# One product for the group moments of two layers in each step of the loop, in place of two

## The chip, the cores and the metric

The kernel runs on one core of a Trainium2 chip. The time is device time in microseconds (us) of one execution on that core. Smaller is better.

## The reference

The input x is 32 images of 16 x 16 tokens with 256 channels, float32. Two residual layers follow each other, each on a group norm of its input (32 groups of 8 channels, with mean and variance over all tokens and channels of a group):

```python
def _gn(v, G=32, eps=1e-05):
    g = v.reshape(B_, H_, W_, G, C_ // G)
    m = jnp.mean(g, axis=(1, 2, 4), keepdims=True)
    s = jnp.var(g, axis=(1, 2, 4), keepdims=True)
    return ((g - m) / jnp.sqrt(s + eps)).reshape(v.shape)

x = x + _L0_conv_ref(_gn(x), ...)
x = x + _L1_conv_ref(_gn(x), ...)
```

Layer 0 is attention in shifted 8 x 8 windows with 16 heads, normalized queries and keys, a position bias, a mask and a softmax. Layer 1 is linear attention with 16 heads, once along the columns of an image (a = 0) and once along the rows (a = 1), and the two results are summed.

## The kernel before

**Layout.** An image lies as [128 channels, 2 x 256 tokens]. Precision comes from pairs of float16 numbers, a high and a low part: ScalarE (ACT) writes the high part, VectorE (DVE) or GpSimd (POOL) the low part (`low`, L1372, and others), and TensorE (PE) multiplies in three passes.

**The order of the work.** Nothing is scheduled by a program. Each engine has its own list of calls, written by hand, with its own waits on semaphores. In the middle each engine runs `step(k)`, which works on about seven images at once, each at another stage: image k enters, image k-1 is in the window attention, k-3 and k-4 in the axial attention, k-6 leaves. PE runs `step(k)` for k = 6 to 31, 26 steps. Hand-ordered lists stand ahead of it and behind it. `reach(eng, sem, img, per, j)` is a wait for the semaphore's count for an image; `edge` is the same wait, but only for the first and the last eight images.

**The group moments.** For an image and a layer, `group_stats` (L1544) and `group_moments` (L1551 to L1554) on DVE leave 12 numbers per channel in `stat[layer]`. `group_means` (L714) on PE multiplies them by the 128 x 128 float32 matrix `group8`, which sums over the eight channels of a group, into 12 columns of a PSUM bank: bank 0 for layer 0, bank 2 for layer 1. `group_var` on DVE reads these sums (L1561) and makes the variance in three more small instructions (L1564, L1566, L1568). `rstd` on POOL (L1377) takes the power -1/2. `group_norm` on DVE (L1580, two instructions for each layer) writes the normalized image in float32.

**One step of PE around it** (L742 to L769): `axial_out(0)` (L661, L662), `group_means(0)` of image k after a wait for `kv_copied[1]` (ACT, L1023), `axial_y` (L672), `group_means(1)` of image k-2, `scores` (L591), `axial_q(1)` and `axial_q(0)` (L559), `axial_out(1)` (L661, L662) after a wait for `biased[1]`, `window_den` (L600), `window_pv` (L609) after a wait for `y_added`, `window_qk` (L559).

**DVE in the same stretch** (end of its step and start of the next): `o1_sum(0)` (L1600), `group_var(0)`, `group_var(1)`, `add_bias` twice (L1660, after the scores), `group_norm(0)`, `group_norm(1)` (L1580), `add_x1` (L1706, L1708), which signals `y_added`.

**POOL in the same stretch** (L1408 to L1423): `rstd(1)`, `rstd(0)`, `token_low(1)` (L1372, kv<-kv, 128 x 1024), `normed_low(0)`:

```python
                for img in there(k - 2):
                    rstd(1, img)
                for img in there(k):
                    rstd(0, img)
                for img in there(k - 3):
                    token_low(1, img)
```

Of the kernel before, what the change touches and what calls it, by code (L numbers as in the profile page):

```python
# [14 lines left out]
P = 128  # L15
# [28 lines left out]
def image(n):  # L44

    return Image(n, n % 2, n // 2, n % 4)


def earlier(img, by):
    return image(img.n - by)  # L50
# [6 lines left out]
def missing(n):  # L57
    return not 0 <= n < IMAGES


def reach(eng, sem, img, per=1, j=None):

    if not missing(img.n):
        eng.wait_ge(sem, img.n * per + (per if j is None else j))
# [10 lines left out]
def placed(usual, moved):  # L75

    return lambda img: moved.get(img.n, usual)


def edge(eng, sem, img, per=1, j=None):  # L80

    if img.n < EDGE or img.n >= IMAGES - EDGE:
        reach(eng, sem, img, per, j)
# [24 lines left out]
def build(nc, x, Wq, Wk, Wv, bv, Wo, bo, logit_scale, cpb_w1, cpb_b1, cpb_w2, w_qkv0, w_out0, w_qkv1, w_out1,  # L108
          c_ident, c_group, c_small, c_mask, c_coords, out, scratch):
    ctx = ExitStack()  # L110
    with ctx:
        def sb(name, shape, dt=F32):
            return ctx.enter_context(nc.sbuf_tensor(name, shape, dt))

        def sem(name):
            return ctx.enter_context(nc.semaphore(name))
# [3 lines left out]
        group8 = sb("group8", [P, P])  # L120
# [20 lines left out]

        x_in = sb("x_in", [P, 2, 2, D])
        x_t = sb("x_t", [P, 2, HALF])
        stat = [sb(f"stat{l}", [P, 32]) for l in range(2)]
        xn32 = [sb(f"xn32_{l}", [P, HALF]) for l in range(2)]
        xn = [sb(f"xn{l}", [P, 2, HALF], F16) for l in range(2)]
        xn1 = [sb("xn_cols", [P, 2, HALF], F16), xn[1]]
# [26 lines left out]
        ps = ctx.enter_context(nc.psum_tensor("ps", [P, 8, 512], F32))  # L174
# [32 lines left out]
        xt_copied = sem("xt_copied")  # L207
        gn_small = [sem(f"gn_small{l}") for l in range(2)]
        gn_sum = [sem(f"gn_sum{l}") for l in range(2)]
        gn_pow = [sem(f"gn_pow{l}") for l in range(2)]  # L210
        xn_hi = [sem(f"xn_hi{l}") for l in range(2)]
        xn_lo = [sem(f"xn_lo{l}") for l in range(2)]
# [16 lines left out]
        v_ready = sem("v_ready")  # L229
# [20 lines left out]
        kv_copied = [sem(f"kv_copied{a}") for a in range(2)]  # L250
# [15 lines left out]

        GN_STEPS = 11
        LATE = 3

        QK_BANK = placed(6, {0: 1, 1: 4})  # L270
        V_BANK = placed(2, {0: 7})
# [16 lines left out]
        GM_BANK = (placed(0, {}),  # L288
                  placed(2, {}))
# [48 lines left out]
        def gram_place(g, s):  # L338

            return 16 * (s // 4 % 2) + 8 * g + 4 * (s // 8) + s % 4  # L340
# [20 lines left out]
        def there(k):  # L361

            img = image(k)
            return [] if missing(img.n) else [img]
# [158 lines left out]
        def _(pe):  # L523
# [130 lines left out]
            def axial_out(a, img):  # L654
                reach(pe, gram_spread[a], img, 64)
                for s in range(G * SEQ):
                    cols = slice(s * SEQ, (s + 1) * SEQ)
                    dst = ps[:, O_BANK[a](img) + s // SEQ, (s % SEQ) * 2 * SEQ:(s % SEQ + 1) * 2 * SEQ]
                    at = gram_place(*divmod(s, SEQ))
                    high, low = (gram_wide[a][:, at, :, :, gp].rearrange("p h e -> p (h e)") for gp in range(2))  # L660
                    pe.matmul(dst.rearrange("p (t i) -> p t i", t=2), high, q1[a][:, :, cols], start=True, stop=False)  # L661
                    last = pe.matmul(dst[:, 0:SEQ], low, q1[a][:, 0, cols], start=False, stop=True)  # L662
                last.then_inc(o1_done[a], 1)

            def axial_y(img):
                reach(pe, o1_lo[1], img)
                for g in range(G):
                    n = 0
                    for a in range(2):
                        for c2 in range(2):  # L670
                            for wp, xp in PASSES:
                                last = pe.matmul(ps[:, Y_BANK(img), g * TOK:(g + 1) * TOK],  # L672
                                                 w_l1[a]["o"][:, wp, c2, g * P:(g + 1) * P],
                                                 o1[a][:, xp, c2 * TOK:(c2 + 1) * TOK],
                                                 start=(n == 0), stop=(n == 11))
                                n += 1
                last.then_inc(y_proj, 1)
# [34 lines left out]
            def group_means(layer, img):  # L712
                reach(pe, gn_small[layer], img, GN_STEPS, 5)
                pe.matmul(ps[:, GM_BANK[layer](img), 0:12], group8[:], stat[layer][:, 0:12],  # L714
                          start=True, stop=True).then_inc(gn_sum[layer], 1)

            def step(k):
                for img in there(k - 4):
                    reach(pe, o1_summed[1], earlier(img, 1))
                    gram_matmuls(0, img)  # L720
                for img in there(k - 3):
                    reach(pe, o_scaled, earlier(img, -1))
                    axial_kv(0, img)
                for img in there(k - 2):
                    window_out(img)
                for img in there(k - 4):
                    reach(pe, gram_lo[0], img)
                    gram_matmuls(1, img)
                for img in there(k - 1):
                    window_v(img)  # L730
                for img in there(k):
                    reach(pe, z_ready, earlier(img, 2))
                    image_channels(img)
                for img in there(k - 3):
                    reach(pe, kv_hi[0], img)
                    axial_kv(1, img)
                for img in there(k - 6):
                    reach(pe, qk_scaled, earlier(img, -5))
                    edge(pe, y_copied, earlier(img, 1))
                    result_rows(img)  # L740
                for img in there(k - 4):
                    reach(pe, xt_copied, earlier(img, -4))  # L742
                    edge(pe, qk_scaled, earlier(img, -3))
                    axial_out(0, img)
                for img in there(k):
                    reach(pe, kv_copied[1], earlier(img, 3))
                    group_means(0, img)
                for img in there(k - 5):
                    edge(pe, kv_copied[1], earlier(img, -2))
                    axial_y(img)  # L750
                for img in there(k - 2):
                    reach(pe, v_ready, earlier(img, -1))
                    group_means(1, img)
                for img in there(k - 1):
                    reach(pe, o1_summed[0], earlier(img, 3))
                    reach(pe, y_copied, earlier(img, 5))
                    scores(img)
                for img in there(k - 3):
                    reach(pe, gn_small[0], earlier(img, -3), GN_STEPS, 6)
                    axial_q(1, img)  # L760
                    reach(pe, gn_small[1], earlier(img, -1), GN_STEPS, 6)
                    axial_q(0, img)
                for img in there(k - 4):
                    reach(pe, biased[1], earlier(img, -3))
                    axial_out(1, img)
                for img in there(k - 1):
                    window_den(img)
                    reach(pe, y_added, earlier(img, 4))
                    window_pv(img)  # L769
                for img in there(k):  # L770
                    window_qk(img)
# [199 lines left out]
        def _(act):  # L971
# [25 lines left out]
            def value_bias_high():  # L997
                act.wait_ge(late_in, 16 * LATE)
                act.activation(bv_two[:, 0, :], bv_col[:], ACT.Copy, scale=WS).then_inc(bv_hi, 1)
# [478 lines left out]
        def _(dve):  # L1478
# [43 lines left out]
            def bias_tables():  # L1522

                dve.wait_ge(rows_in, 16 * 16)
                dve.wait_ge(late_in, 16 * LATE)
                for w in range(NW):
# [29 lines left out]
            def group_var(layer, img):  # L1556

                s, done = stat[layer], gn_small[layer]
                reach(dve, gn_sum[layer], img)
                means = ps[:, GM_BANK[layer](img), 0:12].rearrange("p (g h v) -> p g v h", h=2, v=3)  # L1560
                dve.tensor_reduce(s[:, 20:24].rearrange("p (g v) -> p g v", v=2), means[:, :, 1:3], AXES.X,  # L1561
                                  ALU.add).then_inc(done, 1)
                reach(dve, done, img, GN_STEPS, 6)
                dve.tensor_tensor(s[:, 24:26], s[:, 20:24:2], s[:, 20:24:2], ALU.mult).then_inc(done, 1)  # L1564
                reach(dve, done, img, GN_STEPS, 7)
                dve.tensor_tensor(s[:, 30:32], s[:, 21:24:2], s[:, 24:26], ALU.subtract).then_inc(done, 1)  # L1566
                reach(dve, done, img, GN_STEPS, 8)
                dve.tensor_scalar(s[:, 26:28], s[:, 30:32], 0.0, GN_EPS, ALU.max, ALU.add).then_inc(done, 1)  # L1568
# [385 lines left out]
```

## Time and profile before

| | |
|---|---|
| time, median of 3 runs | 896.25 us (895.89 to 896.89) |
| profiled execution, its own time | 903.6 us |
| its span | 901.4 us |
| PE busy | 844.6 us (94%) |
| DVE busy | 736.4 us (82%) |
| ACT busy | 662.7 us (74%) |
| POOL busy | 480.2 us (53%) |
| granted TensorE clock, mean | 0.978 of full speed |

The span goes from the first to the last instruction of the profiled execution. Busy shares are averages over a start, 26 like steps of 25.5 to 26.6 us each, and an end.

### The profile page before, as it was taken

What the parts mean: (1) busy time and instruction counts of PE and PEld (TensorE: products, weight loads), DVE (VectorE), ACT (ScalarE), POOL (GpSimd) and SP (SyncE); (2) the same over time, 40 slices, a digit from 0 to 9 for tenths busy, and PEclk for the clock granted to TensorE, in tenths of its full rate; (3) what the DMA queues carried; (4) which work ended last, traced back from release to release, by engine and by line L of the source; (5) the groups of instructions that cost most, each with busy time, mean ns of one, the idle gap of its engine ahead of it and who ended that gap; (6) DMA issues with size and microseconds to landing.
All of it is one profiled execution on the core that took longest, in us unless ns stands there. A gap on an engine that the chain in (4) does not pass through costs nothing.

```text
span 901.4 us, 45971 instructions
## 1 busy us (share of the span) xinstructions
PE 844.6 (94%) x20128; PEld 659.9 (73%) x20128; DVE 736.4 (82%) x1536; ACT 662.7 (74%) x1108; POOL 480.2 (53%) x358
## 2 busy tenths in 40 slices
PE   5477899999999999999999999999999999999876
PEld 3354677778788777778787777778777778787655
DVE  7879888888889888888898888888888888887452
ACT  3656777877777778777777787777877877777542
POOL 4445455665655555655655556565565655654220
PEclk9699999999999999999999999999999999999988
DMA  6101434343344443343444443334444343334453
GB/s 165 58 13 36 80 75 81 66 88 78 80 83 92 92 91 82 84 82 81 81 89 92 89 84 81 78 79 87 88 91 92 77 87 77 74 72 94 78 108 83
DMA packets 334430, 74.04 MB, mean 82 GB/s; under 512 B 282372, under 2 KB 333718, under 8 KB 334230
## 3 DMA queue, kind: packets, MB, share of 16 engines
q1 hardware_dynamic: 322128, 69.53, 37.2%
q8 instruction: 158, 2.59, 1.3%
q10 hardware_dynamic: 12102, 1.59, 1.1%
q14 instruction: 42, 0.34, 0.1%
HBM read 12.31 MB, written 8.40 MB: 23 GB/s over the span
## 4 chain that ended last, share of the span: by engine, by line
PE 76%; SPq 7%; DVE 6%; issue 4%; ACT 3%; DMA 2%; POOL 1%; ACTq 1%; DVEq 0%; POOLq 0%
PE ps L559 20%; PE ps L629 15%; PE ps L672 8%; PE ps L661 6%; PE ps L650 6%; PE ps L576 4%; PE ps L662 3%; PE ps L600 3%; PE ps L591 3%; PE ps L609 3%; SPq L439 3%; SPq L429 2%; PE ps L714 1%; PE ps L708 1%; DMA gram_wide<-gram 1%
## 5 line engine op out<-in xcount | busy, mean ns | idle before, releaser
L1372 POOL TENSOR_TENSOR kv<-kv,kv 128x1024 f16<-128x1024 f32 x60 | 128.6, 2144 | 87.1 <-ACT kv L1018 84.3
L1082 ACT ACTIVATE probs<-probs 128x1024 f32<-128x1024 f32 x64 | 67.8, 1059 | 89.5 <-DVE probs L1660 87.4
L1377 POOL TENSOR_TENSOR stat<-stat,small 128x2 f32<-128x2 f32 x64 | 43.3, 693 | 135.5 <-DVE stat L1568 127.8
L661 PEld LDWEIGHTS ps<-q,gram_wide 128*128 128x128 f16 x2048 | 107.2, 97 | 10.9 <-DVE probs L1660 4.9
L661 PE MATMUL ps<-q,gram_wide 128*128 128x32 f16 x2048 | 111.3, 176 | 3.2 <-DMA gram_wide<-gram 2.6
L662 PE MATMUL ps<-q,gram_wide 128*128 128x16 f16 x2048 | 110.4, 169 | 0.0
L662 PEld LDWEIGHTS ps<-q,gram_wide 128*128 128x128 f16 x2048 | 106.0, 97 | 0.4
L559 PE MATMUL ps<-xn,w_q 128*128 128x256 f16 x768 | 98.3, 279 | 6.5 <-POOL xn L1372 6.5
L1594 DVE SCALAR_TENSOR_TENSOR gram<-ps,small,gram 128x512 f16<-128x512 f32 x128 | 94.6, 794 | 8.0 <-ACT gram L1035 5.1
L1372 POOL TENSOR_TENSOR xn<-xn,xn 128x512 f16<-128x512 f32 x64 | 74.9, 1171 | 48.7 <-ACT xn L1071 48.7
L1035 ACT ACTIVATE gram<-ps,small 128x512 f16<-128x512 f32 x128 | 95.4, 818 | 4.4 <-PE ps L650 4.4
L672 PE MATMUL ps<-o,w_o 128*128 128x256 f16 x768 | 90.7, 275 | 2.7 <-DVE o L1606 2.7
L629 PE MATMUL ps<-w_kv,xn 128*128 128x512 f16 x384 | 89.5, 383 | 1.0 <-ACT kv L1023 1.0
L1372 POOL TENSOR_TENSOR qk<-qk 128x1024 f16<-128x1024 f32 x32 | 68.9, 2154 | 38.8 <-ACT qk L1102 38.8
L629 PE MATMUL ps<-w_kv,xn_cols 128*128 128x512 f16 x384 | 88.4, 380 | 0.7 <-DVE o L1600 0.5
L1660 DVE TENSOR_TENSOR probs<-ps,bias_mask 128x1024 f32<-128x1024 f32 x64 | 75.5, 1220 | 14.5 <-PE ps L591 14.5
L559 PEld LDWEIGHTS ps<-xn,w_q 128*128 128x128 f16 x768 | 71.7, 100 | 20.1 <-POOL xn L1372 5.0
L672 PEld LDWEIGHTS ps<-o,w_o 128*128 128x128 f16 x768 | 76.1, 102 | 12.1 <-DVE o L1606 2.9
L1618 DVE STREAM_TRANSPOSE qk<-qk_sq 128x1024 f32<-128x1024 f32 x32 | 39.9, 1245 | 48.4 <-ACT qk_sq L1087 48.4
L1372 POOL TENSOR_TENSOR xn_cols<-xn,xn_cols 128x512 f16<-128x512 f32 x32 | 45.3, 1415 | 58.8 <-ACT xn_cols L1077 58.8
L650 PE MATMUL ps<-v_wide,kv 64*32 64x128 f16 x6144 | 69.2, 224 | 7.5 <-issue 3.7
L650 PEld LDWEIGHTS ps<-v_wide,kv 64*32 64x32 f16 x6144 | 58.8, 90 | 22.3 <-issue 21.1
(124 smaller groups left out, 1976.4 us busy)
## 6 DMA issues: line engine op xcount, KB each, us to landing
gram_wide<-gram SPq DMA_DIRECT2D x248, 128.0 KB
v_wide<-kv SPq DMA_DIRECT2D x496, 32.0 KB
x_in<-x SPq DMA_DIRECT2D x32, 128.0 KB, 2.4
x_in<-x SPq DMA_DIRECT2D x64, 64.0 KB, 2.3
out<-y_out SPq DMA_DIRECT2D x32, 128.0 KB
out<-y_out SPq DMA_DIRECT2D x64, 64.0 KB
gram_wide<-gram ACTq DMA_DIRECT2D x8, 128.0 KB
x<-L_conv_w_qkv SPq DMA_DIRECT2D x1, 768.0 KB, 4.5
```

Of the source, the lines that this page charges most:

```text
L559: last = pe.matmul(dst, w[:, wp, c, m * P:m * P + P], act[:, xp, c * TOK:(c + 1) * TOK], start=(n == 0), stop=(n == 5))
L629: last = pe.matmul(ps[:, KV_BANK[a](img) + t, :], xn1[a][:, xp, c * TOK + t * P:c * TOK + t * P + P], w_l1[a]["kv"][:, wp, c, :], start=(n ...
L650: last = pe.matmul(dst.rearrange("p (s e) -> p s e", e=32), kv[a][rows, kp, t, own], v_wide[a][rows, :, vp, t, own], start=(n == 0), stop= ...
L661: pe.matmul(dst.rearrange("p (t i) -> p t i", t=2), high, q1[a][:, :, cols], start=True, stop=False)
L662: last = pe.matmul(dst[:, 0:SEQ], low, q1[a][:, 0, cols], start=False, stop=True)
L672: last = pe.matmul(ps[:, Y_BANK(img), g * TOK:(g + 1) * TOK], w_l1[a]["o"][:, wp, c2, g * P:(g + 1) * P], o1[a][:, xp, c2 * TOK:(c2 + 1) * ...
L1035: last = act.activation(gram_half(a, head, 0), gram_psum(a, head, img), ACT.Copy, scale=gram_mask[:, head:head + 1])
L1082: act.activation(part, part, ACT.Exp).then_inc(probs_ready[g], 1)
L1372: return pool.tensor_tensor(dst, whole, high, ALU.subtract)
L1377: pool.tensor_tensor(stat[layer][:, 28:30], stat[layer][:, 26:28], minus_half, ALU.pow).then_inc(gn_pow[layer], 1)
L1594: last = dve.scalar_tensor_tensor(gram_half(a, head, 1), gram_psum(a, head, img), gram_mask[:, head:head + 1], gram_half(a, head, 0), ALU. ...
L1660: dve.tensor_tensor(probs[:, 4 * g:4 * g + 4, :].rearrange("p a n -> p (a n)"), ps[:, S_BANK[g](img):S_BANK[g](img) + 2, :].rearrange("p b ...
```

## The change

Both `stat` buffers become one tensor. In PE's `step`, k = 6 to 31, one product `both_group_means` of 24 columns takes the place of the two products of 12; it writes bank 2, where the layer 1 product stood, behind `axial_y`. DVE's `group_var` of both layers waits for it. Products in the hand-ordered lists stay as they are. The wait for `kv_copied[1]` moves to `axial_y`, and the wait of `axial_q(1)` for the layer 0 reader of bank 0 goes.

```diff
-        stat = [sb(f"stat{l}", [P, 32]) for l in range(2)]
+        stat_both = sb("stat", [P, 2, 32])
+        stat = [stat_both[:, l] for l in range(2)]
...
+        TOGETHER = range(6, 32)
+        TOGETHER_BANK = 2
...
+            def both_group_means(img):
+
+                reach(pe, gn_small[0], img, GN_STEPS, 5)
+                reach(pe, gn_small[1], earlier(img, 2), GN_STEPS, 5)
+                pe.matmul(ps[:, TOGETHER_BANK, 0:24], group8[:], stat_both[:, :, 0:12],
+                          start=True, stop=True).then_inc(both_sum, 1)
...
+                for img in there(k - 5):
+                    reach(pe, kv_copied[1], earlier(img, -2))
+                    axial_y(img)
                 for img in there(k):
-                    reach(pe, kv_copied[1], earlier(img, 3))
-                    group_means(0, img)
-                for img in there(k - 5):
-                    edge(pe, kv_copied[1], earlier(img, -2))
-                    axial_y(img)
-                for img in there(k - 2):
-                    reach(pe, v_ready, earlier(img, -1))
-                    group_means(1, img)
+                    reach(pe, v_ready, earlier(img, 1))
+                    both_group_means(img)
...
                 for img in there(k - 3):
-                    reach(pe, gn_small[0], earlier(img, -3), GN_STEPS, 6)
                     axial_q(1, img)
...
-                reach(dve, gn_sum[layer], img)
-                means = ps[:, GM_BANK[layer](img), 0:12].rearrange("p (g h v) -> p g v h", h=2, v=3)
+                k = img.n + 2 * layer
+                if k in TOGETHER:
+                    dve.wait_ge(both_sum, k - TOGETHER.start + 1)
+                    sums = ps[:, TOGETHER_BANK, 12 * layer:12 * layer + 12]
+                else:
+                    dve.wait_ge(gn_sum[layer], k - 2 * layer + 1 if k < TOGETHER.start else k - 2 * layer + 1 - len(TOGETHER))
+                    sums = ps[:, GM_BANK[layer](img), 0:12]
+                means = sums.rearrange("p (g h v) -> p g v h", h=2, v=3)
```

PE in one step, from the product of layer 0 to the first `axial_q`. `ps` is PSUM, `o_0` and `o_1` are the two axial results, `gn_small` counts DVE's small steps of the norm. Before:

```order
L714 MATMUL ps<-stat,group 128x12 [waits gn_small0,kv_copied1]
L672 MATMUL ps<-o_0,w_o 128x256 [waits o1_lo1]
L672 MATMUL ps<-o_0,w_o 128x256 x5
L672 MATMUL ps<-o_1,w_o 128x256 x6
L672 MATMUL ps<-o_0,w_o 128x256 x6
L672 MATMUL ps<-o_1,w_o 128x256 x6
L714 MATMUL ps<-stat,group 128x12 [waits gn_small1,v_ready]
L591 MATMUL ps<-qk,k_two 128x64 [waits y_copied,o1_summed0]
L591 MATMUL ps<-qk,k_two 128x64 x95
L559 MATMUL ps<-xn,w_q 128x256 [waits gn_small0]
```

The same place in the changed kernel, whose lines have other numbers (L676 is `axial_y`, L725 the new product, L595 `scores`):

```order
L676 MATMUL ps<-o_0,w_o 128x256 [waits o1_lo1,kv_copied1]
L676 MATMUL ps<-o_0,w_o 128x256 x5
L676 MATMUL ps<-o_1,w_o 128x256 x6
L676 MATMUL ps<-o_0,w_o 128x256 x6
L676 MATMUL ps<-o_1,w_o 128x256 x6
L725 MATMUL ps<-stat,group 128x24 [waits gn_small1,gn_small0,v_ready]
L595 MATMUL ps<-qk,k_two 128x64 [waits y_copied,o1_summed0]
L595 MATMUL ps<-qk,k_two 128x64 x95
L563 MATMUL ps<-xn,w_q 128x256 x12
```

The layer 0 product ahead of `axial_y` is gone, and the one product left stands behind `axial_y`, with the waits of both.

DVE from `o1_sum(0)` to the bias, before (`group_var(0)` is the first four small instructions, `group_var(1)` the next four):

```order
L1600 TENSOR_TENSOR o_32_0<-ps,o_32_0 128x512 [waits o1_aside0]
L1561 TENSOR_REDUCE stat<-ps 128x4 [waits gn_sum0]
L1564 TENSOR_TENSOR stat<-stat 128x2 [waits gn_small0]
L1566 TENSOR_TENSOR stat<-stat 128x2 [waits gn_small0]
L1568 TENSOR_SCALAR stat<-stat 128x2 [waits gn_small0]
L1561 TENSOR_REDUCE stat<-ps 128x4 [waits gn_sum1]
L1564 TENSOR_TENSOR stat<-stat 128x2 [waits gn_small1]
L1566 TENSOR_TENSOR stat<-stat 128x2 [waits gn_small1]
L1568 TENSOR_SCALAR stat<-stat 128x2 [waits gn_small1]
L1660 TENSOR_TENSOR probs<-ps,bias_mask 128x1024 [waits pv_done,den_done,scores_done] x2
```

The same place in the changed kernel (L1613 is `o1_sum(0)`, L1574 the read of the sums):

```order
L1613 TENSOR_TENSOR o_32_0<-ps,o_32_0 128x512 [waits o1_aside0]
L1574 TENSOR_REDUCE stat<-ps 128x4 [waits both_sum]
L1577 TENSOR_TENSOR stat<-stat 128x2 [waits gn_small0]
L1579 TENSOR_TENSOR stat<-stat 128x2 [waits gn_small0]
L1581 TENSOR_SCALAR stat<-stat 128x2 [waits gn_small0]
L1574 TENSOR_REDUCE stat<-ps 128x4 [waits both_sum]
L1577 TENSOR_TENSOR stat<-stat 128x2 [waits gn_small1]
L1579 TENSOR_TENSOR stat<-stat 128x2 [waits gn_small1]
L1581 TENSOR_SCALAR stat<-stat 128x2 [waits gn_small1]
L1673 TENSOR_TENSOR probs<-ps,bias_mask 128x1024 [waits pv_done,den_done,scores_done] x2
```

No instruction of DVE has moved; the first of the two reads now waits for the common product, `both_sum`.

## Rows read from the trace of the kernel before

**Rows 1.** Page, part 1, and windows view of steps k = 6 to 30

```profile
PE 844.6 (94%) x20128; PEld 659.9 (73%) x20128; DVE 736.4 (82%) x1536; ACT 662.7 (74%) x1108; POOL 480.2 (53%) x358
...
152.50:796.40 643.90, 641.52 (x15704) 506.65 (x15701) 550.92 (x1176) 508.28 (x851) 371.03 (x276) 1.00 0.41 84
```

**Rows 2.** Waits from 152 to 796 us: total us, times, longest

```profile
POOL stat L1377 <- DVE stat L1568: 89.7, 23, 4.8
...
DVE stat L1561 <- PE ps L714: 12.5, 25, 1.0
...
DVE probs L1660 <- PE ps L591: 9.2, 25, 0.5
...
PEld ps L609 <- DVE y L1708: 6.8, 22, 0.4
PEld ps L661 <- DVE probs L1660: 4.7, 20, 0.3
```

**Rows 3.** Timeline of PE's weight loads, one step: start, duration

```profile
408.61 0.30 PEld L714 LDWEIGHTS ps<-stat,group 128*128 128x128 f32 x2
408.74 2.61 PEld L672 LDWEIGHTS ps<-o,w_o 128*128 128x128 f16 x24
411.36 0.30 PEld L714 LDWEIGHTS ps<-stat,group 128*128 128x128 f32 x2
411.69 0.85 PEld L591 LDWEIGHTS ps<-qk,k_two 32*128 32x128 f16 x96
...
417.92 0.95 PEld L609 LDWEIGHTS ps<-probs,v_diag 128*32 128x32 f32 x64 [0.27 <-DVE y L1708]
418.96 0.55 PEld L559 LDWEIGHTS ps<-xn,w_q 128*128 128x128 f16 x6
...
434.25 0.30 PEld L714 LDWEIGHTS ps<-stat,group 128*128 128x128 f32 x2
```

**Rows 4.** Timeline of DVE, the same step

```profile
410.64 0.16 DVE L1561 TENSOR_REDUCE stat<-ps 128x4 f32<-128x8 f32 x1
...
411.80 0.17 DVE L1561 TENSOR_REDUCE stat<-ps 128x4 f32<-128x8 f32 x1 [0.40 <-PE ps L714]
...
412.39 0.17 DVE L1568 TENSOR_SCALAR stat<-stat 128x2 f32<-128x2 f32 x1
412.96 2.36 DVE L1660 TENSOR_TENSOR probs<-ps,bias_mask 128x1024 f32<-128x1024 f32 x2 [0.40 <-PE ps L591]
...
417.59 0.27 DVE L1708 SCALAR_TENSOR_TENSOR y<-ps,x 128x128 f32<-128x128 f32 x1
```

**Rows 5.** Timeline of POOL, the same step

```profile
412.64 1.34 POOL L1377 TENSOR_TENSOR stat<-stat,small 128x2 f32<-128x2 f32 x2 [3.78 <-DVE stat L1568]
413.94 2.14 POOL L1372 TENSOR_TENSOR kv<-kv,kv 128x1024 f16<-128x1024 f32 x1
```

**Rows 6.** First L1580 of two steps, POOL in the second; then both at the start

```profile
415.23 1.00 DVE L1580 TENSOR_SCALAR xn<-x_t,stat 128x256 f32<-128x256 f32 x1
...
261.46 0.88 DVE L1580 TENSOR_SCALAR xn<-x_t,stat 128x256 f32<-128x256 f32 x1
...
260.05 2.14 POOL L1372 TENSOR_TENSOR kv<-kv,kv 128x1024 f16<-128x1024 f32 x1
...
75.28 0.73 DVE L1580 TENSOR_SCALAR xn<-x_t,stat 128x256 f32<-128x256 f32 x2
```

**Rows 7.** Timeline of DVE, a hand-ordered pair of group_var at the start

```profile
52.50 0.17 DVE L1561 TENSOR_REDUCE stat<-ps 128x4 f32<-128x8 f32 x1
...
53.17 0.16 DVE L1561 TENSOR_REDUCE stat<-ps 128x4 f32<-128x8 f32 x1
```

**Rows 8.** Timeline of ACT, the copy that signals kv_copied[1], the same step

```profile
407.53 1.02 ACT L1023 ACTIVATE kv<-ps 128x1024 f32<-128x1024 f32 x1
```

**Rows 9.** Timeline of PE's weight loads, a step whose scores came late

```profile
263.30 0.59 PEld L600 LDWEIGHTS ps<-probs,small 128*32 128x32 f32 x16
264.03 1.07 PEld L609 LDWEIGHTS ps<-probs,v_diag 128*32 128x32 f32 x64
265.19 0.88 PEld L559 LDWEIGHTS ps<-xn,w_q 128*128 128x128 f16 x9
```

More of the change, by code:

```diff
@@ L209, in build @@
         gn_sum = [sem(f"gn_sum{l}") for l in range(2)]
+        both_sum = sem("both_sum")
         gn_pow = [sem(f"gn_pow{l}") for l in range(2)]
```

## The prediction

> **What bounds the kernel now.** I read the page's busy line first, then the windows view of the loop. Over the whole span PE is busy 94%. In the loop it is busy 641.52 of 643.90 us, at a granted clock of 1.00 (its level of 2.4 GHz) [rows 1]. So PE seems to be the bound, and work taken from it seems to be time gained. Matmul records overlap and their ends are modelled, so I check this in the waits. There PE's weight loads wait for two things in nearly every step: `window_pv` (L609) for DVE's `y` in 22 steps, 6.8 us in all, and `axial_out(1)` (L661) for DVE's `probs`, 4.7 us [rows 2]. PE is full, but DVE hands it its work just in time.
>
> Next I follow one step on three engines. PE loads for the layer 0 product at 408.61, for `axial_y` at 408.74, for the layer 1 product at 411.36, for `window_pv` at 417.92, and the next step's first product is at 434.25: a period of 25.64 us [rows 3]. DVE reads the layer 0 sums at 410.64, long after their product, because it was busy; it then stands idle 0.40 us for the layer 1 sums, reads them at 411.80 and ends `group_var(1)` at 412.39 + 0.17 = 412.56 [rows 4]. POOL's two `rstd` start at 412.64, right behind that, and `token_low(1)` at 413.94, until 416.08 [rows 5]. POOL waits for L1568 in the same way 23 times, 89.7 us in all [rows 2].
>
> **The link that decides** is the next one. The first L1580 of `group_norm(0)` starts at 415.23 and takes 1.00 us, where two of them take 0.73 us with no kv subtraction of POOL beside them [rows 6]. It ends at 416.23, 0.15 us after POOL's kv instruction. In the step whose bias came late it starts later and takes only 0.88 us, until 262.34, and POOL's instruction ended at 260.05 + 2.14 = 262.19: 0.15 us again [rows 6]. I find this 0.15 us in all 26 steps. So this DVE instruction does not get through while POOL's large one runs; its end is set by POOL. Behind it DVE is solid until L1708 ends at 417.86, and `window_pv` loads at 417.92 [rows 3, 4]. From the load of the first product to that of `window_pv` are 9.31 us, and within 0.02 us the same in all 26 steps, also where the scores came 0.2 us late.
>
> So the chain of a step is: `kv_copied[1]` (ACT ends at 408.55, PE goes on at 408.61 [rows 3, 8]), product 0, `axial_y`, product 1, `group_var(1)`, `rstd` twice, `token_low(1)`, the norms, `add_x1`, `window_pv`, and from there PE's own work until the next step.
>
> The Trainium skill, "SBUF — State Buffer", section "Who interferes with whom", says that a `tensor_scalar` which can use both ports and a GpSimd instruction exclude each other: whoever is first keeps the shared pair for its whole instruction and the other is fully blocked. The trace agrees, by the constant 0.15 us. By that rule the sum is the one below; were DVE only slowed by sharing, the first rival's sum would hold.
>
> **The change, part by part, in that step.** (1) The layer 0 product goes from its place. `axial_y` loads at 408.61 instead of 408.74: 0.13 us earlier. The wait for `kv_copied[1]` is the same wait at the same time, and costs nothing new. PE's matmul row may gain a little more, so the bounds are 0.13 and, if the whole 0.30 us of the load row [rows 3] went, 0.30. I take 0.13, the distance of the two loads.
> (2) The common product has 24 columns for 12. No row shows this shape. The loads are the same two; 12 more columns are less work than the whole product that stands there now, which with its loads takes 411.69 - 411.36 = 0.33 us [rows 3]. Bounds 0 and 0.33; I take 0.01, since the 0.30 us of loads within the 0.33 do not change.
> (3) `group_var(0)` now waits for the common product. DVE is free at 410.64 [rows 4] and the product's load starts at 411.36 - 0.13 = 411.23, so DVE reads layer 0 at 411.80 - 0.13 + 0.01 = 411.68. `group_var(1)` follows on DVE. In the one place where the two already run back to back, the second read starts 53.17 - 52.50 = 0.67 us after the first [rows 7]. So layer 1 is read at 412.35 instead of 411.80: **0.55 us later**. Bounds: 0.60 (three dependent instructions at the distance of 411.80 to 412.39, with no gap) and 0.80.
> (4) POOL's `rstd(1)` waits for `group_var(1)`, and behind it in POOL's queue are `rstd(0)`, `token_low(1)` and `normed_low(0)`; all but the last move by 0.55, and `token_low(1)` ends at 416.63. The first L1580 ends at 416.78, `add_x1` at 418.41, and `window_pv` loads at 418.47, 0.55 late. `normed_low(0)` waits for the norm and moves by the same.
> (5) DVE's own way is shorter: `group_var(1)` ends at 413.11, the bias starts at about 413.03 (small instructions overlap the next by 0.08 us) for 412.96 [rows 4]. That is 0.07 late, so `axial_out(1)` starts about 0.07 late, and it is hidden behind (4).
> (6) The wait of `axial_q(1)` for bank 0 goes: it was long satisfied, nothing. `axial_q(0)` writes bank 2 after the layer 1 read at 412.35 + 0.17; it came at 413.79 in the trace, nothing. `v_ready` is waited for where it was, 0.13 us earlier; nothing seen.
> (7) PE after `window_pv` is driven by PE, DVE and ACT in turn, none of it tied to the earlier half of the step, so the 0.55 stays. The later `kv_lo[1]` moves SP's v transfers by 0.55 with their readers: nothing.
> (8) What comes back: in about six steps `window_pv` is not late but lasts longer. There the load of `window_den` is at 263.30 and `window_qk` loads 265.19 - 264.03 = 1.16 us after `window_pv` instead of 418.96 - 417.92 = 1.04 [rows 3, 9]. With `window_pv` 0.55 later that 0.12 disappears: 6 x 0.12 = 0.7 us.
>
> **Sum.** 26 steps x 0.55 = 14.3, less 0.7, is +13.6 us. The profiled execution took 903.6 us of its own, which gives 917.2; it stands 7.35 us above the median of the runs. On the median: 896.25 + 13.6 = **909.9 us**, 1.5% slower. By the bounds of (1) to (3): a low of 26 x (0.60 - 0.30) - 0.7 = +7.1 and a high of 26 x (0.80 - 0.13 + 0.33) - 0.7 = +25.3, of which I hold the upper end of (2) very unlikely; with (2) at 0.05 the high is 26 x 0.72 - 0.7 = +18.
>
> **Rivals.** (A) DVE's `group_norm` is not held by POOL, and only DVE's own way counts. Then 0.07 us a step, +1.8 us: 898. Against it: the first L1580 ends 0.15 us behind POOL whenever DVE itself comes. Chance 0.06, half of it within 0.2%.
> (B) Faster. PE, busy 641.52 of 643.90 us, is the bound, and DVE's and POOL's lateness finds room. PE then gains the layer 0 product's place, 0.13 us of the load row up to 0.30 us: 26 x 0.13 = 3.4 to 26 x 0.30 = 7.8 us, about 890.5 in the middle. It decides if `window_pv` could start 0.55 us later at no cost, so if PE came there that late anyway. The wait of 0.27 us before L609 [rows 3] speaks against it. Chance 0.04. The Trainium skill, "Perfetto Trace Analysis", section "Identifying the Most-Contended Engine", would point here: optimize the engine with the highest occupancy first. The same section warns that for TensorE busy matmul time is a poor measure, and the waits in this trace side with the warning.
> (C) The chain is right, but part is given back: DMA waits ahead of `axial_out(0)` in a few steps find more time, or the norm's waits ahead shrink. Half of the effect, +7 us: 903. For it: some steps take 26.0 to 26.6 us instead of 25.6, for reasons beside this chain. Chance 0.10.
> (D) The change does not do what it says: the engines' order shows that it does. Under 0.01.
> My forecast has 0.79.
>
> **How the numbers follow.** The forecast's own range is 906 to 914; (C) lies at 903. The range 902.5 to 914 leaves out A, B and the far tail. A measurement of this kernel can tell about 0.2%, 1.8 us. Slower by more than that: forecast, C and half of A, 0.92; within: 0.04; faster: 0.04.
>
> **What would show it.** In the changed kernel's profile, from `axial_y`'s first load: the product's load 2.6 us later, `window_pv`'s load 9.86 us later (before: 9.31 from the product's load), with a wait for DVE's `y` of about 0.75 us in each step; DVE idle about 1.0 us once a step before the layer 0 read and hardly any before the layer 1 read and the bias; the first L1580 longer, about 1.5 us, and ending 0.15 us after POOL's kv instruction; periods near 26.2 us. The prediction is wrong if `window_pv` still loads at 9.3 us, if the first L1580 ends long after or before POOL's, or if the loop's period grows by less than 0.3 us.

## The result

| | before | changed |
|---|---|---|
| time, median of 6 runs | 897.27 us (895.89 to 899.93) | 906.53 us (903.29 to 909.88) |
| ratio | | 1.0097, 95% interval 1.0066 to 1.0127 |
| loop, k = 6 to 30, in the profiled execution | 643.8 us | 650.6 us |

The changed kernel is about 1% slower. By the ratio that is 8.7 us on 896.25 (5.9 to 11.4).

### The profile page after: what moved, and what is told of

It is laid out like the page before. It is cut to its first block, busy times and chain, and to the rows that moved or that the text cites. A ratio compares the mean times of both kernels' runs of the same rounds, so it can differ in the third digit from the quotient of the medians.

```text
span 901.9 us, 45857 instructions
## 1 busy us (share of the span) xinstructions
PE 842.2 (93%) x20076; PEld 652.1 (72%) x20076; DVE 743.5 (82%) x1536; ACT 665.6 (74%) x1108; POOL 480.3 (53%) x358
## 4 chain that ended last, share of the span: by engine, by line
PE 64%; DVE 18%; issue 8%; SPq 6%; ACT 2%; DMA 1%; POOL 1%; DVEq 0%; ACTq 0%; POOLq 0%
PE ps L633 16%; PE ps L563 14%; PE ps L676 9%; DVE xn L1593 7%; PE ps L654 6%; PE ps L580 4%; PE ps L613 4%; PE ps L665 4%; PE ps L666 2%; DVE probs L1673 2%; SPq L443 2%; PE ps L712 2%; PE ps L702 1%; DVE y L1719 1%; DVE stat L1577 1%
## 5 line engine op out<-in xcount | busy, mean ns | idle before, releaser
L665 PEld LDWEIGHTS ps<-q,gram_wide 128*128 128x128 f16 x2048 | 107.1, 97 | 14.2 <-DVE probs L1673 9.6
L665 PE MATMUL ps<-q,gram_wide 128*128 128x32 f16 x2048 | 111.3, 176 | 5.2 <-DMA gram_wide<-gram 2.6
L676 PE MATMUL ps<-o,w_o 128*128 128x256 f16 x768 | 90.7, 275 | 2.5 <-DVE o L1619 2.3
L676 PEld LDWEIGHTS ps<-o,w_o 128*128 128x128 f16 x768 | 73.7, 99 | 13.9 <-DVE o L1619 2.6
L1673 DVE TENSOR_TENSOR probs<-ps,bias_mask 128x1024 f32<-128x1024 f32 x64 | 75.5, 1219 | 4.3 <-PE ps L595 4.3
L1030 ACT ACTIVATE kv<-ps 128x1024 f32<-128x1024 f32 x60 | 61.4, 1023 | 16.7 <-PE ps L633 16.7
L1379 POOL TENSOR_TENSOR o<-o,o 128x512 f16<-128x512 f32 x60 | 69.7, 1162 | 3.8 <-ACT o L1072 2.7
```

The source lines that it names most:

```text
L1030: act.activation(kv32[a][:], ps[:, KV_BANK[a](img):KV_BANK[a](img) + 2, :], ACT.Copy).then_inc(kv_copied[a], 1)
L1379: return pool.tensor_tensor(dst, whole, high, ALU.subtract)
L1673: dve.tensor_tensor(probs[:, 4 * g:4 * g + 4, :].rearrange("p a n -> p (a n)"), ps[:, S_BANK[g](img):S_BANK[g](img) + 2, :].rearrange("p b ...
```

## The profile after

The page's busy line and the windows view of the loop, in answer to [rows 1] (columns as there):

```profile
PE 842.2 (93%) x20076; PEld 652.1 (72%) x20076; DVE 743.5 (82%) x1536; ACT 665.6 (74%) x1108; POOL 480.3 (53%) x358
...
152.20:802.80 650.60, 641.28 (x15654) 500.17 (x15650) 557.89 (x1176) 510.86 (x851) 371.37 (x276) 1.00 0.41 83
```

PE has 52 matmul records less (26 products of two records) and its loads are 6.5 us less busy in the loop, at the same granted clock of 1.00; and the loop is 6.8 us longer. The waits in the loop, in answer to [rows 2]:

```profile
POOL stat L1384 <- DVE stat L1581: 105.9, 25, 4.4
...
DVE stat L1574 <- PE ps L725: 21.6, 25, 1.0
PEld ps L613 <- DVE y L1721: 18.4, 25, 0.7
...
PEld ps L665 <- DVE probs L1673: 9.2, 24, 0.5
```

`window_pv` (now L613) waits 18.4 us for DVE's `y`, where it waited 6.8. One step of PE's loads, in answer to [rows 3] (L676 `axial_y`, L725 the common product):

```profile
411.99 2.52 PEld L676 LDWEIGHTS ps<-o,w_o 128*128 128x128 f16 x24
414.52 0.30 PEld L725 LDWEIGHTS ps<-stat,group 128*128 128x128 f32 x2
414.85 0.87 PEld L595 LDWEIGHTS ps<-qk,k_two 32*128 32x128 f16 x96
...
421.75 0.94 PEld L613 LDWEIGHTS ps<-probs,v_diag 128*32 128x32 f32 x64 [0.73 <-DVE y L1721]
```

From the place of `axial_y`'s load to `window_pv` are 9.76 us, before 9.31 from the product that stood there. DVE in the same step, in answer to [rows 4] (L1574 reads the sums, L1581 ends a `group_var`, L1673 is the bias; L1593 is the first normalization alone):

```profile
414.96 0.17 DVE L1574 TENSOR_REDUCE stat<-ps 128x4 f32<-128x8 f32 x1 [0.84 <-PE ps L725]
...
415.63 0.16 DVE L1574 TENSOR_REDUCE stat<-ps 128x4 f32<-128x8 f32 x1
...
416.22 0.17 DVE L1581 TENSOR_SCALAR stat<-stat 128x2 f32<-128x2 f32 x1
416.32 2.36 DVE L1673 TENSOR_TENSOR probs<-ps,bias_mask 128x1024 f32<-128x1024 f32 x2
...
418.60 1.47 DVE L1593 TENSOR_SCALAR xn<-x_t,stat 128x256 f32<-128x256 f32 x1
...
421.42 0.28 DVE L1721 SCALAR_TENSOR_TENSOR y<-ps,x 128x128 f32<-128x128 f32 x1
```

And POOL, in answer to [rows 5]:

```profile
416.46 1.34 POOL L1384 TENSOR_TENSOR stat<-stat,small 128x2 f32<-128x2 f32 x2 [4.21 <-DVE stat L1581]
417.77 2.15 POOL L1379 TENSOR_TENSOR kv<-kv,kv 128x1024 f16<-128x1024 f32 x1
```

The idle time of DVE now stands in front of the layer 0 read, the layer 1 read follows 0.67 us later, and POOL is held back with it. Its kv instruction ends at 419.92; the first normalization, begun at 418.60, ends at 420.07, again 0.15 us behind. In all 26 steps of both profiles the distance is 0.15 us.

The table has, for each kernel of this study, medians over the 25 periods from k = 6 to k = 30, worked out from the start times of such rows, in us from the start of the loads that follow `axial_out(0)`: the end of POOL's `token_low(1)`, the end of the first normalization, the end of `add_x1`, the load of `window_pv`, that of `window_qk`, and the period.

| kernel | token_low(1) end | first norm end | add_x1 end | window_pv | window_qk | period |
|---|---|---|---|---|---|---|
| before | 7.48 | 7.63 | 9.27 | 9.32 | 10.35 | 25.64 |
| changed | 7.93 | 8.08 | 9.71 | 9.77 | 10.80 | 25.95 |
| short_low_before | 5.54 | 6.97 | 8.61 | 9.09 | 10.31 | 25.58 |
| short_low_after | 5.98 | 7.01 | 8.65 | 9.12 | 10.34 | 25.72 |
| two_products_late | 7.92 | 8.07 | 9.70 | 9.76 | 10.79 | 25.97 |
| one_var_one_rstd | 6.95 | 7.10 | 8.73 | 8.95 | 10.18 | 25.52 |
| one_var_two_rstd | 7.27 | 7.42 | 9.06 | 9.11 | 10.21 | 25.52 |
| merged_biased0 | 6.95 | 7.10 | 8.73 | 8.88 | 10.10 | 25.51 |
| before_biased0 | 7.48 | 7.63 | 9.26 | 9.32 | 10.35 | 25.62 |
| after_rstd0_first | 7.29 | 7.44 | 9.08 | 9.14 | 10.36 | 25.63 |
| before_rstd0_first | 6.82 | 6.98 | 8.61 | 9.10 | 10.32 | 25.69 |
| after_low_later | 12.17 | 7.02 | 8.65 | 9.16 | 10.37 | 27.61 |
| before_low_later | 12.13 | 6.97 | 8.61 | 9.25 | 10.47 | 27.40 |

The spans of single profiled executions (901.4 and 901.9 us) hide the difference: from the start of step k = 31 to the end, where the two kernels differ only in that one step, they took 105.0 and 99.1 us, and the thirteen profiles of this study lie between 99.1 and 106.3 there. The granted clock in that stretch was 0.92 and 0.96 in the two, but it does not put the thirteen in order (before_rstd0_first has 103.0 us at 0.97, merged_biased0 99.5 us at 0.93); what makes it differ is open. The ratios below come from several runs each, against runs of the kernel before on the same chip.

## Experiments

**short_low_before and short_low_after: POOL's long instruction cut.**

```diff
-                low(kv[a][:, 1], kv32[a][:], kv[a][:, 0]).then_inc(kv_lo[a], 1)
+                n = 2 if a == 1 and 3 <= img.n <= 28 else 2 * D
+                low(kv[a][:, 1, :, 0:n], kv32[a][:, :, 0:n], kv[a][:, 0, :, 0:n]).then_inc(kv_lo[a], 1)
```

> The kernel before, with POOL's token_low(1) of images 3 to 28 cut to 2 of 512 columns for each half, so it ends about 0.7 us after its start instead of 2.14 us; the rest of the low part of kv of layer 1 is left out, so it holds old values. Theory (POOL's long instruction holds the first L1580 and with it window_pv): the first L1580 no longer lasts 1.0 us but 0.4, add_x1 ends about 0.7 us earlier, and window_pv loads at about 9.0 us from the step's first product instead of 9.32, where PE's own work is the next limit; its matmuls can start only 0.05 to 0.1 us earlier, so the time is 1 to 3 us below the kernel before. Rival (DVE's own way sets window_pv): the first L1580 and window_pv stay where they are, no change.

> The changed kernel with the same cut of token_low(1) (the rest of that low part is left out). Theory: without POOL's long instruction the later rstd costs nothing. The first L1593 starts when the bias ends, about 6.6 us after axial_y's load, and lasts 0.4 us; window_pv loads near 9.1 instead of 9.77; the whole loss of about 0.45 us a step goes: 896 us, within 3 us of the kernel before, and 9 to 12 us below the changed kernel. Rival (the loss is on DVE or PE itself: more small instructions behind one product): it stays at 905 to 908 us.

Measured: short_low_before 0.9986 of the kernel before (0.9968 to 1.0004), short_low_after 0.9988 (0.9966 to 1.0010). A step of short_low_before, DVE's two norms of layer 0, then POOL, then PE's load:

```profile
414.95 0.73 DVE L1581 TENSOR_SCALAR xn<-x_t,stat 128x256 f32<-128x256 f32 x2
```

```profile
413.73 0.20 POOL L1372 TENSOR_TENSOR kv<-kv,kv 128x4 f16<-128x4 f32 x1
...
417.46 1.13 PEld L609 LDWEIGHTS ps<-probs,v_diag 128*32 128x32 f32 x64
```

With POOL out of the way two norms take 0.73 us together, as at the start of the kernel [rows 6]. The load of `window_pv` has no wait any more. In short_low_after the late `rstd` is still there and costs nothing that can be measured: the loss of the change is gone (`window_pv` at 9.12 us, 9.09 in short_low_before). POOL's short form took 0.20 us, not the 0.7 I had put down; nothing hangs on that. The rival, that DVE or PE loses the time by itself, falls.

**two_products_late: the place alone.**

```diff
+                for img in there(k - 5):
+                    reach(pe, kv_copied[1], earlier(img, -2))
+                    axial_y(img)
                 for img in there(k):
-                    reach(pe, kv_copied[1], earlier(img, 3))
                     group_means(0, img)
-                for img in there(k - 5):
-                    edge(pe, kv_copied[1], earlier(img, -2))
-                    axial_y(img)
```

> The kernel before with only the place changed: both products stay, with 12 columns each, but the layer 0 product stands behind axial_y, right ahead of the layer 1 product. Theory (the loss comes from where the layer 0 sums arrive, not from merging): group_var(0) is read at about 2.97 us from axial_y's load and group_var(1) 0.67 us later, as in the changed kernel; the second product's 0.33 us on PE hide behind window_pv's wait. 905 to 908 us, the same as the changed kernel. Rival (the merged product of 24 columns, or its double wait, is what costs): within 3 us of the kernel before.

Measured: 1.0082 (1.0062 to 1.0103); this ratio and the changed kernel's 1.0097 each lie within the other's interval. DVE's reads of the sums in one step, and PE's loads:

```profile
416.68 0.17 DVE L1560 TENSOR_REDUCE stat<-ps 128x4 f32<-128x8 f32 x1 [0.83 <-PE ps L714]
417.35 0.16 DVE L1560 TENSOR_REDUCE stat<-ps 128x4 f32<-128x8 f32 x1
```

```profile
423.48 0.94 PEld L609 LDWEIGHTS ps<-probs,v_diag 128*32 128x32 f32 x64 [0.58 <-DVE y L1707]
```

Two products behind `axial_y` cost what one does there. So the loss is where the layer 0 sums arrive, and the product saved on PE has no price: it hides in the wait before `window_pv`.

**after_rstd0_first and before_rstd0_first: POOL's order of the two rstd.**

```diff
-                for img in there(k - 2):
-                    rstd(1, img)
                 for img in there(k):
                     rstd(0, img)
+                for img in there(k - 2):
+                    rstd(1, img)
```

> The changed kernel with one swap on POOL: rstd(0) stands ahead of rstd(1) in the step. Theory: rstd(0) no longer waits for group_var(1), it runs on POOL while DVE makes group_var(1), so the two rstd end about 0.65 us earlier, token_low(1) runs from about 5.15 to 7.3 us instead of 5.78 to 7.93, the first L1593 ends near 7.45 instead of 8.08, add_x1 near 9.07, and window_pv loads at about 9.15 instead of 9.77 (9.32 in the kernel before, which has 0.14 us less in front). 10 to 14 us below the changed kernel, 0 to 4 us below the kernel before. Rival (the loss is one product's late sums on DVE, whatever POOL does): no change, 905 to 908 us.

> The kernel before with the same swap. Theory: rstd(0) runs before group_var(1) ends, token_low(1) starts at about 4.70 us from the first product instead of 5.34, the first L1580 ends near 7.0 instead of 7.63, and window_pv loads at 9.09, where PE's own work is the limit (as in short_low_before): 0 to 3 us faster than the kernel before. Rival: no change of the first L1580's end.

Measured: after_rstd0_first 0.9985 (0.9968 to 1.0003), before_rstd0_first 1.0012 (0.9988 to 1.0035). POOL in one step of after_rstd0_first:

```profile
415.42 1.37 POOL L1384 TENSOR_TENSOR stat<-stat,small 128x2 f32<-128x2 f32 x2 [3.73 <-DVE stat L1581]
416.75 2.14 POOL L1379 TENSOR_TENSOR kv<-kv,kv 128x1024 f16<-128x1024 f32 x1
```

Here all work is done and only POOL's order differs. Its step began at 411.60, so the kv instruction starts at 5.15 us instead of 5.78. The loss is gone, by the same amount as with the cut instruction. In the kernel before the swap moves every term as expected too (`add_x1` ends at 8.61), but PE takes over as the limit at 9.10, and `window_qk`, 1.22 us behind it instead of 1.03, is 0.03 us early only: no gain that can be measured. The 0.2 us before `window_pv` in the kernel before were not worth having, the 0.45 us more were.

**one_var_one_rstd and one_var_two_rstd: the merging completed.** In the loop one `group_var` of four DVE instructions works on both layers; the first of the two kernels has one `rstd` as well.

```diff
+                dve.wait_ge(both_sum, k - TOGETHER.start + 1)
+                means = ps[:, TOGETHER_BANK, 0:24].rearrange("p (x h v) -> p x v h", h=2, v=3)
+                dve.tensor_reduce(s[:, :, 20:24].rearrange("p l (g v) -> p l g v", v=2), means[:, :, 1:3], AXES.X,
+                                  ALU.add).then_inc(both_var, 1)
...
+                        pool.tensor_tensor(stat_both[:, :, 28:30], stat_both[:, :, 26:28],
+                                           minus_half.unsqueeze(1).to_broadcast([P, 2, 2]), ALU.pow).then_inc(both_pow, 1)
```

> The changed kernel with the rest of the chain merged too: in the steps k = 6 to 31 one group_var of four DVE instructions and one rstd on POOL serve both layers. Theory: group_var ends at 2.97 + 0.76 = 3.73 us from axial_y's load, rstd is one instruction of 0.68 us, token_low(1) runs from about 4.46 to 6.6, and the first normalization ends near 6.75 instead of 8.08. Then PE's own way is the limit, with the layer 0 product and its place gone: window_pv 0.2 to 0.3 us earlier than in the kernel before in each of 26 steps, 888 to 892 us. Rival (the bias, not the norm, sets window_pv, and one product has no gain for it): 895 to 897 us.

> As one_var_one_rstd, with one group_var for both layers but the two rstd instructions of the changed kernel. Theory: group_var ends at 3.73 us from axial_y's load, two rstd of 0.65 us follow, token_low(1) starts at about 5.12 instead of 4.80, the first normalization ends near 7.4, add_x1 near 9.05, window_pv at about 9.1 instead of 8.95. So 0.1 to 0.2 us a step slower than one_var_one_rstd, 0.1 to 0.5% faster than the kernel before. Rival (DVE's four instructions less do nothing, all of the gain is the merged rstd): as slow as the changed kernel.

Measured: one_var_one_rstd 0.9946 (0.9918 to 0.9974), one_var_two_rstd 0.9955 (0.9930 to 0.9980). POOL in one step of the first:

```profile
412.49 1.01 POOL L1409 TENSOR_TENSOR stat<-stat,small 128x4 f32<-128x4 f32 x1 [3.73 <-DVE stat L1604]
413.47 2.13 POOL L1402 TENSOR_TENSOR kv<-kv,kv 128x1024 f16<-128x1024 f32 x1
```

Both beat the kernel before by about 0.5%: for one_var_one_rstd the low side of what I expected, for one_var_two_rstd the high side. The merged `rstd` of 4 columns takes 1.01 us, against 1.34 for two of 2 columns, so it saves 0.33 us where I had counted on about 0.65, and its share of the gain is too small to tell from none (0.9946 against 0.9955, intervals overlapping). The expected gap of 0.1 to 0.2 us a step between the two is there at `window_pv` (8.95 and 9.11) and gone at `window_qk` (10.18 and 10.21). So of the step from the changed kernel to these two, nearly all comes from the DVE instructions saved. Against the kernel before two things are in the gain, and no run separates them: the scores load 2.86 us into the step instead of 3.08, since the product and its place are gone, and the bias can follow them (at 4.17 and 4.18 us, before 4.28), since DVE is free for it. In the changed kernel it started at 4.34.

**before_biased0 and merged_biased0: another wait of PE.** `axial_out(1)` needs only the bank that `add_bias(0)` reads.

```diff
-                    reach(pe, biased[1], earlier(img, -3))
+                    reach(pe, biased[0], earlier(img, -3))
```

> The kernel before with the same wait moved from biased[1] to biased[0] in the loop, nothing else. Theory: the wait of 0.21 us before axial_out(1) goes, and window_den comes earlier, but window_pv still waits for add_x1, whose end POOL's token_low(1) sets: window_pv stays at 9.32 us from the first product and the time within 1 us of the kernel before. Rival (PE's start of axial_out(1) sets the step): 0.2 us a step, 5 us faster.

> As one_var_one_rstd, and axial_out(1) waits for biased[0] instead of biased[1] in the loop (it writes banks 3 and 4; of the scores' banks it shares only bank 4, which add_bias(0) has read by then). In one_var_one_rstd PE waited 0.22 us a step there for DVE's probs, and window_pv then came with PE's own pace at 8.95 us, add_x1 ending at 8.73. Theory (with the norm's chain short, PE and this wait are the limit): axial_out(1) starts at about 6.3 instead of 6.58, window_pv loads at about 8.8, limited by add_x1 at 8.73: 0.1 to 0.2 us a step, 3 to 5 us below one_var_one_rstd, 7 to 10 us below the kernel before. Rival (window_pv is set elsewhere): no change against one_var_one_rstd.

Measured: before_biased0 0.9999 (0.9976 to 1.0022), merged_biased0 0.9939 (0.9920 to 0.9958). PE's loads in before_biased0 wait for DVE's `y` longer than before:

```profile
PEld ps L609 <- DVE y L1708: 10.3, 25, 0.5
```

In the kernel before, a wait of about 0.2 us a step can be taken from PE and nothing is won: PE waits 10.3 us instead of 6.8 ahead of `window_pv`, whose load stays at 9.32 us, as the theory has it. With the norm's chain short, 0.07 us of it reach `window_pv` and 0.08 us `window_qk`; the 3 to 5 us that I expected over one_var_one_rstd did not come (0.9939 against 0.9946 is no difference). One reason is seen further on in the step. From the load of `result_rows` to that of `axial_out(0)` PE now takes 19.8 us in the sum of the 25 periods, 16.3 in one_var_one_rstd; in eight steps the profile has it wait there for the transfers `gram_wide<-gram` (in three steps in one_var_one_rstd). At 0.6% below the kernel before, merged_biased0 has the lowest ratio of the study, by no measurable distance.

**after_low_later and before_low_later: the long instruction moved away.**

```diff
-                for img in there(k - 3):
-                    token_low(1, img)
                 for img in there(k):
                     normed_low(0, img)
+                for img in there(k - 3):
+                    token_low(1, img)
```

> The changed kernel with one swap in POOL's step: token_low(1) stands behind normed_low(0) instead of ahead of it; all work is done. Theory: POOL's long instruction no longer lies beside the first L1593, which then starts with the end of the bias at 6.6 us and lasts 0.4; window_pv loads near 9.1 instead of 9.77, so 8 to 11 us are won against the changed kernel, unless the later kv low part makes gram_matmuls(1) or axial_kv(0) of the next step wait, which would give back up to half. Rival (the loss is in PE's or DVE's own order): no change or slower.

> The kernel before with the same swap in POOL's step. Theory: the first L1580 starts with the end of the bias and lasts 0.4 us, window_pv loads at about 9.09 as with the short low part, limited by PE: 0 to 3 us faster than the kernel before, less what the later kv low part costs. Rival: no change of the first L1580's end.

Measured: 1.0590 (1.0542 to 1.0638) and 1.0569 (1.0535 to 1.0604). In the part that I aimed at the expectation holds (first norm at 7.02, `window_pv` at 9.16). But the kv low part is now done 4.24 us later, and PE asks for what is made from it as early as ever. Waits of PE in after_low_later:

```profile
PE ps L654 <- DMA v_wide<-kv: 28.1, 23, 2.3
PE ps L665 <- DMA gram_wide<-gram: 11.3, 22, 1.0
```

and the SP queue in one of its steps:

```profile
408.19 14.19 SPq L443 DMA_DIRECT2D v_wide<-kv  x16
422.42 1.77 SPq L465 DMA_DIRECT2D out<-y_out  x3
424.24 3.67 SPq L433 DMA_DIRECT2D gram_wide<-gram  x4
```

`gram_matmuls(1)` waits for the v transfers. SP issues the gram transfers only behind them in these rows, so `axial_out` waits too. I had allowed for half of the gain to be given back; over 50 us were lost against the kernel before. I had asked who waits for that instruction's result, but not by how much its transfers were early.

## Why the prediction was right

Its numbers: 909.9 forecast, 902.5 to 914 as the range, 906.53 measured, slower as forecast. The chain and its price at `window_pv` are right; the sum is too large, +13.6 us where the ratio gives +8.7 (5.9 to 11.4).

- **The bound.** Right. PE, busy nearly all of the loop, waits for DVE's `y` in every step, and 6.5 us less of weight loads bought nothing.
- **The link.** That POOL's `token_low(1)` sets the end of the first normalization is shown: by the constant 0.15 us at five different ends of that instruction (6.95, 7.27, 7.29, 7.48 and 7.93 in the table), by its absence when the instruction is cut, and by POOL's order alone. Where DVE came later than POOL had finished (short_low) it took 0.40 us. The two numbers give one rule that holds in all 26 steps of the eleven kernels with `token_low(1)` in its place, within 0.01 us: the first normalization ends 0.40 us after its own start or 0.15 us after POOL's end, whichever is later. So the last 0.25 us of POOL's record cost DVE nothing: in before_rstd0_first the normalization starts 0.05 to 0.30 us before POOL's end, and up to 0.25 us it still takes 0.40. Whether POOL lets go that much ahead of the end of its record, or the first part of DVE's instruction needs nothing that POOL holds, is not shown. The rule of the Trainium skill that the prediction weighed, "SBUF — State Buffer", section "Who interferes with whom", full blocking and no sharing, agrees with this: overlaps from 0.27 to 1.33 us all end at the same 0.15 us. For a `tensor_scalar` the section ties it to the modes that use both ports, and no run here shows which mode this instruction ran in. Rival (A), 898 us, is out.
- **(1)** The product's place was mis-sized. The common product loads 2.53 us after `axial_y`'s load, not 2.62: `axial_y`'s 24 loads themselves take 2.52 instead of 2.61 us [rows 3]. So 0.22 us came off where I had 0.13.
- **(2)** Right: 0.33 us from the product's load to the next (414.52 to 414.85), and DVE reads 0.44 us after it, both as with 12 columns. I had 0.01 more.
- **(3)** Right: 415.63 - 414.96 = 0.67 us. With (1), layer 1 is read at 3.64 instead of 3.19: 0.45 us late, not 0.55.
- **(4)** The path is right: 0.45 us at `token_low(1)`, at the first norm and at `window_pv`, in all 26 steps, and at `window_qk` by the median. (5) too: the bias starts 0.05 us late (medians), and it stays hidden.
- **(7) and (8)** Here the sum failed most: (7) let nothing come back behind `window_pv`, and (8) gave back 0.7 us. Over the 25 periods `window_pv` comes 244.2 - 233.0 = 11.2 us later in sum. From there to `window_qk` 2.0 us come back (28.0 to 26.0), and 2.4 us more between `window_qk` and the next step (382.8 to 380.4): 6.8 us remain.
  - The 2.0 us: in the kernel before, `window_pv` lasts 0.1 to 1 us longer than its shortest form in 7 of 25 steps, in the changed kernel in 1. The longer wait before it is not the reason: short_low_before, which has no such wait, has 2, and one_var_two_rstd has 12. What makes them is open.
  - The 2.4 us: `gram_matmuls` is longer than its shortest form in 20 of 50 cases before and in 11 after, 1.2 us less in sum, and the time from the load of `result_rows` to that of `axial_out(0)` falls from 16.2 to 14.3 us; 0.8 us are lost again in `axial_out(0)`. The waits of PE ahead of `axial_out(0)`, in the kernel before (L661) and then in the changed one (L665, one wait in all; "issue" means that the profile names no releaser):

```profile
PEld ps L661 <- issue: 2.3, 5, 1.0
...
PE ps L661 <- DMA gram_wide<-gram: 1.2, 2, 0.8
```

```profile
PEld ps L665 <- issue: 0.2, 1, 0.2
```

In two of the five steps the profile names the gram transfers. This is what case (C) had: such waits find more time when PE comes later. The two kernels with `window_pv` at 9.76 and 9.77 us, changed and two_products_late, are the lowest in both numbers (11 and 10 of 50 cases, 14.3 and 14.1 us); the nine others with `token_low(1)` in its place have 17 to 27 cases and 15.0 to 19.8 us. So part of the delay is bought back behind `window_pv` each time. `scores`, which stands ahead of the wait, was longer more often in the changed kernel (16 of 25 steps, before 9), at no cost.

The sum with measured terms: 26 x 0.45 = 11.7, less 4.4 x 26 / 25 = 4.6, is 7.1 us, against 8.7 (5.9 to 11.4) from the ratio. So a fifth of each step's price was not there (0.45 for 0.55 us, nearly all of it by the product's place in (1)), and 4.6 us came back where 0.7 were counted. The range held because it reached down to (C). One sign of being wrong was met by one way of counting: the period was to grow by at least 0.3 us, and it grew by 0.31 in the median and by 6.8 / 25 = 0.27 in the mean. Rival (B) had the right saving on PE, up to 7.8 us, and no way for it to reach the end.

## What to carry to other kernels

Before merging two small instructions, ask who waits for the first result alone: here the early half kept DVE's small steps out of the chain, and the saved TensorE work had no price as long as DVE's small steps stayed unmerged. When results are merged, merge the steps behind them too, which turned 1% of loss into 0.5% of gain here, or let the result that is ready first go first in the next queue, which turned it into none. Ahead of each wait of the busiest engine look at what else touches the instruction that ends it: a long GpSimd instruction beside it can be the real bound. And before an instruction is moved back, measure how early its result is now for each reader, transfers and the queue behind them included.

## What was unexpected of the hardware

- A run of 24 weight loads (float16, 128 x 128) took 2.61 us behind a float32 product's loads and 2.52 us without one in front; the cause is not shown.
- An overlap of up to 0.25 us between DVE's normalization and POOL's kv instruction cost nothing; every further part of it was paid in full.
- GpSimd's power took 0.69 us for 128 x 2 elements and 1.01 us for 128 x 4, so its cost is not a fixed one. Its subtraction took 0.20 us for 128 x 4 and 2.14 us for 128 x 1024.
- The 16 v transfers of one step took SP 14.19 us to issue in after_low_later, the waits among them included.
